# A twelve-block network on one core: fourth block's keys in four quarters, seventh block's key weights folded into the queries, key tiles moved to the norms, loads cut in parts

## What is computed

```
L1_xattn: q = query Wq; k = key Wk; v = value Wv            (128 features)
          qh = q wq_h + bq_h; kh = k wk_h + bk_h; vh = v wv_h + bv_h   (8 features)
          scores = qh kh' / sqrt(8); where(mask, -1e9, scores); softmax; @ vh; tile 16 times; @ Wo
L2_xattn: qp = q Wq' + bq; kp = k Wk' + bk; vp = v Wv' + bv
          softmax(qp kp' / sqrt(128)) @ vp
L3_xattn: keys = context Wkv[:, :1024], each head of 64 divided by its norm
```

## Time and profile before

| | us |
|---|---|
| median of three runs | 1204.77 |
| lowest and highest | 1202.14, 1205.06 |
| profiled execution, its own time | 1201.56 |
| its span, first to last instruction | 1199.8 |
| TensorE busy | 1061.1 (88%) |
| VectorE, ScalarE, GpSimd busy | 516.1, 462.5, 422.4 |
| mean granted TensorE clock | 0.932 |

### The profile page before, as it was taken

How to read it: one execution, slowest core, us unless ns; L and a number is a source line. 1 busy time by engine, 2 the same in 40 slices (tenths; PEclk the granted TensorE clock), 3 DMA queues, 4 the chain that set the end, 5 groups by cost and what they waited for, 6 DMA issues and landing times.

```text
span 1199.8 us, 18789 instructions
## 1 busy us (share of the span) xinstructions
PE 1061.1 (88%) x8004; PEld 695.2 (58%) x8004; DVE 516.1 (43%) x906; ACT 462.5 (39%) x726; POOL 422.4 (35%) x198
## 2 busy tenths in 40 slices
PE   5797898989889998889789969999999999999458
PEld 3685443645677885346468835555655565565334
DVE  3234762134433333622342345445545544643444
ACT  2474614333325664234332034434344334433111
POOL 1352110001014553010110007786877677776000
PEclk9899999996889998799979969999999999999769
DMA  8532000031003333010650032132112322210200
GB/s 333 219 136 83 36 36 0 1 140 53 1 37 123 146 156 141 11 42 1 244 228 39 3 139 70 71 104 107 71 71 74 112 98 71 70 71 1 77 1 9
DMA packets 20771, 102.76 MB, mean 86 GB/s; under 512 B 1744, under 2 KB 1744, under 8 KB 18896
## 3 DMA queue, kind: packets, MB, share of 16 engines
q1 hardware_dynamic: 20688, 101.57, 21.8%
HBM read 67.75 MB, written 33.82 MB: 85 GB/s over the span
## 4 chain that ended last, share of the span: by engine, by line
PE 83%; DVE 8%; ACT 4%; issue 2%; DMA 1%; POOL 1%; POOLq 0%; DVEq 0%; ACTq 0%
PE PSUM L2180 19%; PE PSUM L2106 10%; PE PSUM L1536 9%; PE PSUM L1689 3%; PE PSUM L1546 3%; PE PSUM L1724 3%; PE PSUM L1831 2%; PE PSUM L1842 2%; PE PSUM L1733 2%; PE PSUM L1786 2%; PE PSUM L2222 1%; PE PSUM L2039 1%; PE PSUM L2029 1%; PE PSUM L1632 1%; PE PSUM L2010 1%
## 5 line engine op out<-in xcount | busy, mean ns | idle before, releaser
L469 POOL TENSOR_TENSOR CK<-CK,ARENA 128x2048 f32<-128x2048 f32 x63 | 285.1, 4526 | 123.3 <-ACT ARENA L788 119.2
L2180 PE MATMUL PSUM<-ARENA,CT 128*128 128x512 f32 x512 | 238.7, 606 | 0.0
L1377 DVE TENSOR_TENSOR ARENA<-PSUM,RK 128x512 f32<-128x512 f32 x256 | 159.0, 684 | 183.8 <-PE PSUM L2106 183.8
L788 ACT ACTIVATE ARENA<-ARENA,WB 128x1024 f32<-128x1024 f32 x128 | 147.3, 1151 | 200.6 <-DVE ARENA L1377 198.0
L2106 PEld LDWEIGHTS PSUM<-ARENA 64*128 64x128 f32 x2048 | 119.4, 188 | 51.0 <-issue 47.0
L2180 PEld LDWEIGHTS PSUM<-ARENA,CT 128*128 128x128 f32 x512 | 91.3, 189 | 98.6 <-issue 90.5
L389 POOL TENSOR_TENSOR RSTD<-VE,MHALF 128x4 f32<-128x4 f32 x17 | 17.1, 1008 | 347.7 <-DVE VE L863 285.0
L1536 PE MATMUL PSUM<-CT,WK 128*128 128x128 f32 x1024 | 139.0, 284 | 0.0
L2106 PE MATMUL PSUM<-ARENA 64*128 64x128 f32 x2048 | 131.8, 278 | 2.7 <-ACT WB L783 2.2
L1536 PEld LDWEIGHTS PSUM<-CT,WK 128*128 128x128 f32 x1024 | 129.0, 199 | 8.4 <-issue 6.1
L410 POOL TENSOR_TENSOR W<-KEYS 128x512 f32<-128x512 f32 x28 | 36.6, 1307 | 113.0 <-ACT KEYS L492 63.8
(11 more groups left out here) (392 smaller groups left out, 1470.9 us busy)
## 6 DMA issues: line engine op xcount, KB each, us to landing
ARENA<-kept_keys SPq DMA_DIRECT2D x16, 2048.0 KB, 8.0
kept_keys<-KEYS SPq DMA_DIRECT2D x32, 512.0 KB, 2.7
kept_keys<-W SPq DMA_DIRECT2D x32, 512.0 KB, 2.6
CT<-in_ctxT SPq DMA_DIRECT2D x4, 1024.0 KB, 10.5
CK<-in_l0f_experts SPq DMA_DIRECT2D x1, 4096.0 KB, 22.7
CK<-in_ctxk SPq DMA_DIRECT2D x1, 4096.0 KB, 12.0
ARENA<-in_l2f_experts SPq DMA_DIRECT2D x2, 2048.0 KB, 7.1
CT<-in_ctxk SPq DMA_DIRECT2D x1, 4096.0 KB, 14.2
```

What stands on the lines that cost most here:

```text
L469: nc.gpsimd.tensor_tensor(LS[b % 2], LS[b % 2], PR[:, t % 2, :], ALU.add)\
L788: act(p, p, ACT.Exp, bias=SHIFT).then_inc(sem("l3x_probs"), AC.sends("l3x_probs"))
L1377: ve.tensor_tensor(PR[:, k, q * 512:(q + 1) * 512].rearrange("p (j n) -> p j n", j=4), bank(q).rearrange("p (j n) -> p j n", j=4), each(rk ...
L2180: last = mm(bank(4 + q), CTK[:, t, :], PR[:, t % 2, q * 512:(q + 1) * 512], start=k == 0, stop=k == KEY_TILES - 1)
```

## The change

Five edits go together.

1. **Fourth block in quarters.** The context keys of one row b are four quarters of 512 tokens at partitions 0, 32, 64, 96 of one bank, made by four 8-column products side by side; four evictions instead of sixteen. The folded query product is made four times, at the same partitions, and a score product reads quarter c at partitions 32c to 32c + 8. The products no longer wait for l0a's result.
2. **Mask as a limit.** LIMIT is 3e38 where a token is kept and -1e9 where it is masked; one minimum replaces the multiplication and the addition. LIMIT is built inside the expert loop of l0f, behind expert 2, no longer ahead of l1x's norm. The next row's scores now wait for that minimum (`long_taken`), not for the shift.
3. **Seventh block.** The key weight multiplies the queries (`l2x_Wk`, one 512-column product and a copy to TMP) and the scores read the context itself, CT; the key bias comes back as one number per query (four products of one column, LKB), which VectorE adds to and subtracts from the maximum. All sixteen context-key products and their copies go.
4. **Long loops.** Context products follow their turned group: turn 0, turn 1, contexts 0, turn 2, contexts 1, turn 3, contexts 2 and 3.
5. **Key tiles and loads.** Tiles: l0f_norm 1, l1x_norm 2, l1f_norm 2, l2x_norm 2 are new places, l1x has 2 (was 3), l1a 22 (was 28). SyncE's loads are cut: WB in 6 parts and the experts in 8, each issued behind a key store of l0x; `ctxk` in 4 parts behind the stores of the two l1x_norm and two l1x tiles. The last load of l2f's experts and WC are issued behind the l2f stores (they were ahead of l2a's).

```diff
-        for place, n in (("l0x", L0X_TILES), ("l0a", 3), ("l0a_scan0", 2), ("l0a_scan1", 2), ("l1x", 3), ("l1a_norm", 2), ("l1a", 28),
-                         ("l1f", 2), ("l2x", 1), ("l2a", 2), ("l2f", 4)):
+        for place, n in (("l0x", L0X_TILES), ("l0a", 3), ("l0a_scan0", 2), ("l0a_scan1", 2), ("l0f_norm", 1), ("l1x_norm", 2), ("l1x", 2),
+                         ("l1a_norm", 2), ("l1a", 22), ("l1f_norm", 2), ("l1f", 2), ("l2x_norm", 2), ("l2x", 1), ("l2a", 2), ("l2f", 4)):
...
+            for t in range(places["l0f_norm"][-1] + 1):
+                keep_keys(t)
+                if t < WB_PARTS:
+                    load_part(WB, d["wb"], "dma_wb", t, WB_PARTS)
...
+                elif t <= WB_PARTS + EXPERT_PARTS:
+                    load_part(CK[:, :, :].rearrange("p a b -> p (a b)"), d["l0f_experts"], "dma_experts", t - WB_PARTS - 1, EXPERT_PARTS)
             nc.sync.wait_ge(sem("x_ready"), SP.due("x_ready", n=3))
-            load(CK[:, :, :], d["ctxk"], "dma_ck")
-            keep_keys("l1x", "l1a")
+            for n, t in enumerate(range(places["l1x_norm"][0], places["l1a"][-1] + 1)):
+                keep_keys(t)
+                if n < CK_PARTS:
+                    load_part(CK[:, :, :].rearrange("p a b -> p (a b)"), d["ctxk"].rearrange("p a b -> p (a b)"), "dma_ck", n, CK_PARTS)
...
                 s = SL[:, b % 2, :]
-                ve.tensor_tensor(s, PSUM[:, 0:4, :].rearrange("p c n -> p (c n)"), KEEP, ALU.mult)\
-                    .then_inc(sem("dve_step"), DV.sends("dve_step"))
-                nc.vector.wait_ge(sem("dve_step"), DV.sent("dve_step"))
-                ve.tensor_tensor(s, s, NEG, ALU.add).then_inc(sem("dve_step"), DV.sends("dve_step"))
-                nc.vector.wait_ge(sem("dve_step"), DV.sent("dve_step"))
+                ve.tensor_tensor(s, PSUM[:, 0:4, :].rearrange("p c n -> p (c n)"), LIMIT, ALU.min)\
+                    .then_inc(sem("long_taken"), DV.sends("long_taken"))
...
+                        if masked:
+                            r = slice(32 * c, 32 * c + HD)
+                            last = mm(PSUM[:, c, :], QT[r, b * P:(b + 1) * P], KT1[r, b * 512:(b + 1) * 512], start=True, stop=True)
+                        else:
+                            last = mm(PSUM[:, c, :], TMP[:, b * P:(b + 1) * P], CT[:, b * S + c * 512:b * S + (c + 1) * 512],
...
-            nc.tensor.wait_ge(sem("x_ready"), PE.due("x_ready", n=2))
             nc.tensor.wait_ge(sem("l1x_product_kept"), PE.due("l1x_product_kept"))
             keys_settled(places["l0a_scan1"][-1], places["l0a_scan1"][-2])
-            context_keys_pe(WKK, HD, 0, CHUNKS // 2)
+            for b in range(B):
+                if b >= 2:
+                    nc.tensor.wait_ge(sem("context_keys_kept"), b - 1)
+                for c in range(4):
+                    last = mm(PSUM[32 * c:32 * c + HD, 1 + b % 2, :], WKK, CT[:, b * S + c * 512:b * S + (c + 1) * 512],
+                              start=True, stop=True, skip_group_check=True)
+                last.then_inc(sem("context_keys"), PE.sends("context_keys"))
+            make_before_turn("l0f_norm", (4, 5, 6))
...
-            context_keys_pe(w("l2x_WkT"), c0=CHUNKS // 2)
+            make_before_turn("l2x_norm", (3, 4, 1))
...
+            mm(bank(6), w("l2x_Wk"), QT[:, :], start=True, stop=True).then_inc(sem("q_rows"), PE.sends("q_rows"))
```

More of the change, by code:

```diff
@@ L34 @@
 FAR = -1.0e30
+NO_LIMIT = 3.0e38
 SAFE_EXPONENT = 60.0
@@ L343, in _ @@
             load(ROWS[:, :], d["rows"].broadcast_to([P, d["rows"].shape[1]]), "dma_rows")
-            load(WB[:, :], d["wb"], "dma_wb")
-            load(MASK8[:, :], d["mask"], "dma_mask")
-            load(IDX[:, :], d["idx"].broadcast_to([P, 8]), "dma_idx")
-            load(CK[:, :, :].rearrange("p a b -> p (a b)"), d["l0f_experts"], "dma_experts")
-            def keep_keys(first, last):
-                for t in range(places[first][0], places[last][-1] + 1):
-                    nc.sync.wait_ge(sem("keys_kept"), 2 * t + 2)
-                    sync.dma_start(d["keys"][t], KEEP_T[t % 2]).then_inc(sem("dma_keys%d" % (t % 2)), 16)
@@ L354, in _, with load_part, keep_keys @@
-            keep_keys("l0x", "l0a_scan1")
+            def load_part(dst, src, signal, k, parts):
+                n = dst.shape[1]
+                at, end = n * k // parts, n * (k + 1) // parts
+                load(dst[:, at:end], src[:, at:end], signal)
+            def keep_keys(t):
+                nc.sync.wait_ge(sem("keys_kept"), 2 * t + 2)
+                sync.dma_start(d["keys"][t], KEEP_T[t % 2]).then_inc(sem("dma_keys%d" % (t % 2)), 16)
+            for t in range(places["l0f_norm"][-1] + 1):
+                keep_keys(t)
+                if t < WB_PARTS:
+                    load_part(WB, d["wb"], "dma_wb", t, WB_PARTS)
+                elif t == WB_PARTS:
+                    load(MASK8[:, :], d["mask"], "dma_mask")
+                    load(IDX[:, :], d["idx"].broadcast_to([P, 8]), "dma_idx")
+                elif t <= WB_PARTS + EXPERT_PARTS:
+                    load_part(CK[:, :, :].rearrange("p a b -> p (a b)"), d["l0f_experts"], "dma_experts", t - WB_PARTS - 1, EXPERT_PARTS)
@@ L360, in _ @@
             load(ARENA[:, 14336:14336 + 4 * NW], d["l2f_experts"][:, 0:4 * NW], "dma_moe8_early")
-            keep_keys("l1f", "l2x")
+            for t in range(places["l1f"][0], places["l2x"][-1] + 1):
+                keep_keys(t)
             nc.sync.wait_ge(sem("x_ready"), SP.due("x_ready", n=2))
+            for t in places["l2a"]:
+                keep_keys(t)
             load(ARENA[:, 4096:4096 + 4 * NW], d["l2f_experts"][:, 4 * NW:8 * NW], "dma_moe8")
+            for t in places["l2f"]:
+                keep_keys(t)
@@ L972, in _ @@
             tail_dve()
-            nc.vector.wait_ge(sem("dma_wb"), DV.due("dma_wb"))
+            nc.vector.wait_ge(sem("dma_wb"), DV.due("dma_wb", n=WB_PARTS))
             norm_twice_dve()
@@ L1950, in _ @@
             nc.tensor.wait_ge(sem("q_rows_kept"), PE.due("q_rows_kept"))
-            nc.tensor.wait_ge(sem("context_keys_kept"), 32)
-            long_pe(P, False)
+            mm(bank(6), w("l2x_Wk"), QT[:, :], start=True, stop=True).then_inc(sem("q_rows"), PE.sends("q_rows"))
+            for b in range(B):
+                last = mm(PSUM[:, 7, b:b + 1], QT[:, b * P:(b + 1) * P], w("l2x_bk"), start=True, stop=True)
+            last.then_inc(sem("l2x_key_bias"), PE.sends("l2x_key_bias"))
+            nc.tensor.wait_ge(sem("q_rows_kept"), PE.due("q_rows_kept"))
+            keys_settled(places["l2x_norm"][-1], places["l2x_norm"][-1] - 1)
+            long_pe(False)
             nc.tensor.wait_ge(sem("long_z_kept"), 8)
@@ L2291, in lay_out @@
     down, up = i["L1_ffn_W_down"], i["L1_ffn_W_up"]
+    four = lambda v: col(np.tile(np.pad(v, (0, 32 - HD)), 4))
     wqkv, bqkv = i["L1_attn_Wqkv"], i["L1_attn_bqkv"]
```

164 lines of the change are left out of this document (97 added, 67 removed).

## The result

The changed kernel takes **1151.16 us** in the median of 4 executions (1148.87 to 1160.85), the kernel before 1204.87 in the same comparison. The ratio is 0.9575, 95% interval 0.9519 to 0.9631: 4.3% faster, some 51 us. Forecast were 1137 and 68 us, with a range up to 1153. The median alone lies inside that range; the ratio, which goes by all executions, puts the change at 1153.7, just outside it. So the direction was right, the forecast gain a third too large, and the range too narrow on that side.

The account below looks back on a forecast made before the run. TensorE, on the last chain for 83% of the span, was taken as the bound. Terms 10.8 + 2.1 + 32.1 + 18.2 + 4.7 + 0.4 - 2 = 66.3 us off 1201.56 gave 1135.3, adjusted towards the median to 1137 us; range 1126 to 1153.

Parts of the forecast that it names:

- Loads in parts: In l0x, the stall for the late key store and the slow steps behind it go: 10.8 us gained, bounds 0 and 10.8.
- l0f: Context keys side by side take 3.6 us, not 7.33, and the turn comes earlier: 2.1 us gained, bounds 0 and 3.6.
- rival B: In l0f's context keys and the scores, side-by-side forms do not overlap: 21 us more, 1158 us; chance 0.06.
- l1x: Fourth block ends at 305.2, not 337.33, with passes of 7.0 set by ScalarE: 32.1 us gained, bounds 22 and 34.
- l1a: Six steps go from two key tiles to one, 6.85 to 3.81 us each: 18.2 us gained, bounds 16 and 18.2.
- l1f: The turn, behind the context keys at 480.5 before, comes at 475.8: 4.7 us gained, bounds 0 and 6.4.
- l2x: Context-key products leave, a projection is added, passes grow from 10.2 to 10.5: 0.4 us gained, bounds -3 and +3.
- Later stages: Behind l2x, later loads are due 30 us after their new place: cost 0.
- Clock: New gaps in l1x can bring the half clock level back for a stretch: 2 us lost.
- Rival C: Half clock through the fourth block, 6.7 us of a pass becoming 12: +12 over half the block, 1149 us; chance 0.10.

Follow-up runs that it names:

- x1: The kernel before with one edit, the weights, mask and l0f's experts loaded in parts between l0x's key stores: 1194.96 us, ratio 0.9933.
- x3: The changed kernel with ctxk loaded in two parts instead of four: 1150.35 us, ratio 0.9548.
- x6: The changed kernel with all four turns of a pass ahead of the context products again, in l1x and l2x: 1146.43 us, ratio 0.9541.

## Why the prediction was off, step by step

- **Loads in parts**, 10.8: 8.8 at the turn of l0x's result, 8.4 in x1. The stall went as told. Missing are 2 us, most of it a stretch at 1.2 GHz in the first steps (26 to 30 us). Another 0.9 us was lost from there to l0a's turn, which no term held.
- **l0f**, 2.1: 2.8 from l0a's turn to l0f's, of which some 1.7 is a shorter half-clock stretch in the scan. The side-by-side form does 16 products of 512 columns in 3.76 us, forecast 3.6; rival B is out.
- **l1x**, 32.1: 26.7 (from l0f's turn to the products behind the last row: 146.2 us before, 119.5 now). The norm's scaling took 1.84 us and not 1.11; queries took 6.4 and not 5.4 us, partly at 1.2 GHz. Scores took 1.14, forecast 0.9. The first exponential, 8.4 us behind the scores, was forecast at 8.7. The wait for ctxk was 2.99, forecast 1.6 (bounds 0 and 5), and the half-clock stretch behind it is the larger miss: the first pass took 11.9 us, forecast 8.6. Later passes are 7.19 and 7.18, forecast 7.0, with the last turn released by ScalarE as told. The wait of 2.31 us before the first turn was forecast, as 2.4.
- **l1a**, 18.2: 14.8. Steps have the forecast lengths but for the one of 9.70 us, 2.85 more at 1.2 GHz. x3, without that stretch, has 17.8.
- **l1f**, 4.7: 5.7.
- **l2x**, 0.4: -2.7. The program is 57.8 us ahead at l1f's turn, 59.7 at l2x's and 55.1 at l2a's. Passes are 10.45, as forecast; the second scores at 1.2 GHz cost 3.1, the whole of the miss. x6 shows that the pass need not have grown.
- **Later stages**, 0: -4.2, the unchanged work with 12 us more at 1.2 GHz.
- **Clock**, an allowance of 2: this step failed. The stages' terms took the stretches of before at 39 to 50, 264 to 316 and 465 to 476 us as gone, 54 us at 1.2 GHz. Some 6 were given back, 4 by the allowance and 2 in l1f's pair. Measured, the sum went from 163 to 156. The work was forecast well: in the profiled pair it fell by 47.5 us (1120.0 to 1072.5), where my sum, less the clock's part of about 24, held some 42. So the clock's part fell short by some 20 us, and work that was forecast too small hid 5 of them.

Rival C had half clock in the fourth block alone, at 1149 us and a chance of 0.10. That is close to the time measured, but for the wrong places: the fourth block holds 5 us of the shortfall, the rest lies in l0x, l1a, l2x and behind. My range took each place by itself and never asked how much time at 1.2 GHz the whole program would have left.

By the Trainium skill, "TensorE: Matmul & The Clock Gate", Measured speedup vs the span model, four row tiles gain 3.07 times. The four scores went from 3.70 to 1.14 us, 3.2 times, nearer to the page than to the four that I took. The four column groups of the context keys gain 3.9 times (2 x 7.33 against 3.76), as the row of l1a's products had said. So row groups and column groups did not gain alike here, and a row of column groups was a poor witness for the scores; why they differ no run shows.
